# Wide attention: key blocks weighed in pairs, and all projections of a unit at its last block

## The chip, the cores and the metric

The kernel runs on one core of a Trainium2 chip. The metric is the device time of one launch in microseconds (us). The core has engines that run side by side and are ordered only by semaphores: TensorE (PE, matmuls into PSUM, with PEld for the loads of its stationary operand), VectorE (DVE), ScalarE (ACT), GpSimd (POOL), and SyncE (SP), which issues DMAs here.

## The reference

Four layers, each an attention-like part and a feed-forward part with layer norms between. The change touches the attention of the last layer alone ("wide": 16 heads of 64 channels, 4 sequences of 1024 tokens, 128 channels):

```python
def _L3_attn_ref(x, adaptive_scale, Wq, bq, Wk, bk, Wv, bv, Wo, bo, gamma, beta):
    H, HD, D = (16, 64, 128)
    Q = (x @ Wq.T + bq).reshape(B, N, H, HD)
    K = (x @ Wk.T + bk).reshape(B, N, H, HD)
    V = (x @ Wv.T + bv).reshape(B, N, H, HD)
    scores = jnp.einsum('bnhd,bmhd->bhnm', Q, K)
    scores = scores * (SCALE * adaptive_scale)[None, :, None, None] / TEMP
    w = jax.nn.softmax(scores, axis=-1)
    attn = jnp.einsum('bhnm,bmhd->bnhd', w, V).reshape(B, N, H * HD)
    y = x + (attn @ Wo.T + bo)
    ...                       # layer norm, times gamma, plus beta
```

## The kernel before

The wide stage is `wide_attention` (L4147). It works through 32 units, one for each sequence and pair of heads (4 x 8). The two heads of a pair lie in partitions 0 to 63 and 64 to 127. A unit has 8 key blocks (kb) of 128 keys, and each block two halves (h) of 512 queries.

One Python list, `plan`, sets the order of the work (L4234 to L4275). Every engine walks through the same list and does its own part of each step, so a step's place in the list is its place in each engine's queue. The steps:

- `score` (PE L4370 and L4373): for one block and half, the negated row maxima are added by a bf16 matmul with ones, then the fp32 product of keys and queries; two heads side by side (64 rows each). ScalarE takes the exponential of the whole tile (L4511) into one of 6 buffers.
- `max` (PE L4065, DVE L4096): bf16 scores of the *next* unit, and their maxima; 16 of them in a unit, spread over the blocks by `MAXIMA`.
- `weigh` (PE L4387): values times exponentials of one block, both halves, into two PSUM banks of its own that are kept through the unit; 64 output columns for each head.
- `add` (DVE, h = 0) and `add_beside` (POOL, h = 1), both L4304: the running sum of the exponentials. A list `waiting` holds the adds that GpSimd has still to do; `beside` takes one from it and puts it behind a `max`, for whose matmuls GpSimd then waits.
- `send` (DVE L4104, PE L4072, DVE L4109 and L4111, then four DMAs L4121): the negated maxima of the next unit, turned and stored as rows for its scores.
- `project_q`, `project_k` (PE L4056; ACT L4130, and L4139 with L4143) and `project_v` (PE L4051, DVE L4086): for the unit after the next.
- `keep` (ACT L4519), `sums` (PE L4398, ACT L4525, DMAs L4325), `invert` (DVE L4444, DMAs), `divide` (DVE L4439): the end of the unit before.
- `rows` (L269) and the norms' steps for a whole sequence: `next_step(True)` gives a heavy one, `next_step(False)` a light one. `gate_work` gives two pieces of the router's bisection (small VectorE steps, L3897 to L3963, `PIECES` = 9 + 8 x 25 + 6 of them) in each block but the last.

Three PSUM slots of two banks are handed round in turn by `with_banks` (L113): `score`, `max`, `send`, the projections, `sums`, `rows` and the turns each take the next one, and TensorE waits until the step that had it three takes before has been read out. An exponential waits until its buffer, used six tiles before, was weighed and added:

```python
if t >= E_BUFS:
    a_.wait_ge(*weighted.at(t - E_BUFS + 1))
    a_.wait_ge(*summed[t % HALF].at(add_of(t - E_BUFS)))
```

Of the kernel before, what the change touches and what calls it, by code (L numbers as in the profile page):

```python
# [10 lines left out]
NT = T // P  # L11
# [101 lines left out]
def with_banks(plan, n, released):  # L113


    out, done, at = [], [None] * n, -1
    for step in plan:
        if step[0] in released:
            at = (at + 1) % n
            out.append((step, at, done[at]))  # L120
            done[at] = released[step[0]](*step[1:])
        else:
            out.append((step, None, None))
    return out
# [3845 lines left out]
class WideHeads:  # L3970
# [3 lines left out]
    SLOTS, TILES, PRODUCTS, N_LOADS = 3, HALF * NT, 12, 8  # L3974
# [172 lines left out]
def wide_attention(core, heads, sort, tail):  # L4147
# [11 lines left out]
    own, units, SLOTS, TILES = heads.own, heads.units, heads.SLOTS, heads.TILES  # L4159
# [9 lines left out]
    sums = core.arena[:, ArenaBuffers.COLS - T - BANK:ArenaBuffers.COLS - T]  # L4169
# [31 lines left out]
    work, ends, later = [], [], []  # L4201
    rest = [moe.steps(1)] + [gathered(b) + moe.steps(b) for b in range(2, nb)]

    def gate_work(n):
        return [work.pop(0) for _ in range(min(n, len(work)))]

    def finish(b):
        ends.extend(("rows", 2 * b + i) for i in range(HALF))
        if b + 1 < nb:
            rest.insert(len(rest) - 1 if b == 0 else len(rest), [(False, None)] + mine.steps(b) +  # L4210
                        [(False, ("route",))] * (b == 0))
        else:
            later.extend([("stats_1", b), ("root_1", b), ("scale_1", b, 0), ("scale_1", b, 1),
                          ("affine", b, 0), ("affine", b, 1), ("affine", b, 2), ("stats_2", b),
                          ("root_2", b), ("scale_2", b, 0), ("scale_2", b, 1)])
            later.extend(("turn", 2 * b + i) for i in range(HALF))

    def next_step(heavy):

        while rest and not rest[0]:  # L4220
            rest.pop(0)
        if not rest or rest[0][0][0] != heavy:
            return []
        step = rest[0].pop(0)[1]
        if step == ("route",):
            work.extend([("gate",)] * Entmax.PIECES)
        return [step] if step else []

    waiting = []

    def beside(step):
        return [("add_beside", *waiting.pop(0), step)] if waiting else []

    plan = []  # L4234
    for u in range(len(units)):
        todo = list(range(TILES)) if u + 1 < len(units) else []
        for kb in range(NT):
            for h in range(HALF):
                plan.append(("score", u, kb, h))
                for _ in range((MAXIMA[kb] + h) // HALF if todo else 0):  # L4240
                    plan.append(("max", u + 1, todo.pop(0)))
                    plan += beside(plan[-1])
            plan += beside(None)
            if kb == NT - 1 and u + 1 < len(units):
                plan.append(("send", u + 1))
            if kb == NT - 1:
                more = u + 2 < len(units)
                plan += [("project_k", u + 2)] * more + next_step(True) + [("project_v", u + 2)] * more
            if kb:
                plan += [("weigh", u, kb - 1), ("add", u, kb)]  # L4250
                waiting.append((u, kb))
                if kb == NT - 2:
                    plan += next_step(True) + [("project_q", u + 2)] * (u + 2 < len(units))
            elif u:
                plan += [("weigh", u - 1, NT - 1), ("keep", u - 1)]
            if kb < NT - 1:
                plan += gate_work(IN_TILE)
            if kb < NT - 2:
                plan += next_step(False)
            if u and kb == 1:  # L4260
                plan.append(("sums", u - 1))
            elif u and kb == 3:
                plan.append(("invert", u - 1))
            elif u and kb == 5:
                plan.append(("divide", u - 1))
                if units[u - 1][1] == PAIRS - 1:
                    finish(units[u - 1][0])
            if kb >= NT - 2 and ends:
                plan.append(ends.pop(0))
    assert not work and not any(rest) and not ends  # L4270
    last = len(units) - 1
    plan += beside(None)
    plan += [("weigh", last, NT - 1), ("keep", last), ("sums", last), ("invert", last), ("divide", last)]
    finish(nb - 1)
    plan += ends + later  # L4275
    plan = with_banks(plan, 3, {
        "score": lambda u, kb, h: (exped, TILES * u + HALF * kb + h + 1),
        "sums": lambda u: (sums_kept, u + 1),
        "rows": lambda c: rows.left(c),
        "turn": lambda c: (turn.kept, c + 1),  # L4280
        "n_turn": lambda tag, c: (norms[tag].turn.kept, c + 1),
        "route": lambda: (entmax.router.done, 1), **heads.released()})
# [446 lines left out]
def build(nc, inp, const, out, n_batch):  # L4729
    core = Core()  # L4730
    core.nc, core.inp, core.const, core.out, core.n_batch = nc, inp, const, out, n_batch
    with ExitStack() as ctx:
# [49 lines left out]
        wide = WideHeads(core)  # L4782
        block_experts(core, sort, tail, wide)
        wide_attention(core, wide, sort, tail)
        wide.st.close()
        tail.st.close()
# [42 lines left out]
```

## Time and profile before

| | |
|---|---|
| median of 3 runs | 5642.71 us (5641.98 to 5645.2) |
| profiled execution, its own time | 5626.77 us |
| its span in the trace | 5625.0 us |
| TensorE busy | 5183.8 us (92%) |
| VectorE busy | 3972.7 us (71%) |
| ScalarE busy | 2760.5 us (49%) |
| GpSimd busy | 1340.1 us (24%) |
| wide stage | about 3593 to 5072 us |
| `score` exponentials, L4511 | 512 of 1.02 us |
| `max` reductions, L4096 | 496 of 1.22 us |

Busy times are unions of instructions of one engine. "Idle before" is the time in which an engine had nothing to do ahead of a group, with what ended it. TensorE's ends are modelled, so its pace is better read from the starts of its instructions; a wait of its own can stand with PEld, whose weight load goes first.

### The profile page before, as it was taken

How to read it: one execution, taken by the hardware profiler on the slowest of the kernel's cores; microseconds unless marked ns; L12 is line 12 of the kernel's file. 1: busy time of each engine (PE TensorE's matmuls, PEld its weight loads, DVE VectorE, ACT ScalarE, POOL GpSimd, SP SyncE). 2: the span in 40 equal slices, each digit the busy share in tenths (PEclk: the TensorE clock that was granted, in tenths of full speed). 3: DMA queues.
4: the chain of work that ended last, by engine and by line, in shares of the span. 5: the costliest groups of instructions: out<-in, count | busy, mean ns of one | idle time of the engine just before them, and what ended most of it. 6: DMA issues, size and time to landing. Idle time of an engine off the chain costs nothing. (4 is left out here: it accounts for less than half of the span.)

```text
span 5625.0 us, 103745 instructions
## 1 busy us (share of the span) xinstructions
PE 5183.8 (92%) x40013; PEld 2672.4 (48%) x40013; DVE 3972.7 (71%) x6826; ACT 2760.5 (49%) x4661; POOL 1340.1 (24%) x933
## 2 busy tenths in 40 slices
PE   6999997787999999998999979899999999997999
PEld 2333333444567777773333339433433434335676
DVE  7888886774567677777998944578688787864312
ACT  4767666221233333336786866454454454442333
POOL 0120100230112322322112214155344343440000
PEclk7999999787999999999999989999999999998999
DMA  4212110002111111111122113000000000001000
GB/s 91 49 33 32 33 32 12 0 0 63 37 33 25 30 26 30 26 30 31 27 39 38 42 51 88 29 20 17 13 13 20 9 13 13 13 16 35 5 5 8
DMA packets 148427, 158.08 MB, mean 28 GB/s; under 512 B 48980, under 2 KB 95108, under 8 KB 147508
## 3 DMA queue, kind: packets, MB, share of 16 engines
q1 hardware_dynamic: 143336, 142.37, 11.6%
q0 software_dynamic: 4096, 8.40, 0.5%
q8 instruction: 318, 5.21, 0.4%
q14 instruction: 173, 1.42, 0.1%
q10 hardware_dynamic: 504, 0.69, 0.1%
HBM read 118.20 MB, written 37.40 MB: 28 GB/s over the span
## 5 line engine op out<-in xcount | busy, mean ns | idle before, releaser
L4096 DVE TENSOR_REDUCE wide_max_parts<-wide_p 128x2 f32<-128x1024 f32 x496 | 595.2, 1220 | 130.0 <-PE wide_p L4065 117.9
L795 ACT ACTIVATE attn_w<-l_p 128x512 f32<-128x512 f32 x1024 | 553.4, 595 | 229.7 <-DVE l_p L1241 115.7
L2594 PE MATMUL caus_p<-caus_x_one,big 128*128 128x129 f32 x4608 | 634.1, 284 | 0.0
L641 DVE TENSOR_REDUCE l_max_parts<-l_p 128x2 f32<-128x1024 f32 x512 | 601.8, 1218 | 44.3 <-PE l_p L617 40.5
L2678 ACT ACTIVATE big<-caus_p 128x512 f32<-128x512 f32 (+3 forms) x768 | 345.9, 489 | 544.7 <-PE caus_p L2580 399.7
L641 DVE TENSOR_REDUCE rot_max_parts<-rot_p 128x2 f32<-128x1024 f32 x488 | 574.1, 1219 | 46.3 <-PE rot_p L617 43.1
L2594 PEld LDWEIGHTS caus_p<-caus_x_one,big 128*128 128x128 f32 x4608 | 585.1, 197 | 35.6 <-issue 2.3
L4373 PE MATMUL wide_p<-arena 64*128 64x512 f32 x2048 | 530.2, 596 | 0.0
L4511 ACT ACTIVATE attn_w<-wide_p 128x1024 f32<-128x1024 f32 x342 | 350.4, 1024 | 333.8 <-PE wide_p L4373 332.5
L4304 POOL TENSOR_TENSOR big<-big,attn_w 128x1024 f32<-128x1024 f32 x128 | 333.5, 2605 | 392.8 <-PE wide_p L4065 380.9
L641 DVE TENSOR_REDUCE caus_max_parts<-caus_p 128x2 f32<-128x1024 f32 (+2 forms) x360 | 340.4, 956 | 24.2 <-PE caus_p L617 15.9
L772 PE MATMUL l_p<-l_q_stack,l_k_stack 98*32 98x512 bf16 x4096 | 342.9, 388 | 5.8 <-ACT attn_w L795 4.2
L2712 POOL TENSOR_TENSOR attn_w<-attn_w,caus_part 128x256 f32<-128x256 f32 x256 | 185.7, 725 | 677.4 <-DVE caus_part L2652 677.4
L4387 PE MATMUL wide_p<-attn_w,arena 128*64 128x512 f32 x1368 | 332.0, 606 | 0.0
L772 PE MATMUL rot_p<-arena 98*32 98x512 bf16 x4096 | 319.6, 386 | 6.3 <-ACT big L795 2.1
L795 ACT ACTIVATE attn_w<-rot_p 128x512 f32<-128x512 f32 x512 | 275.5, 596 | 88.3 <-PE rot_p L772 87.6
L3333 ACT ACTIVATE arena<-moe_experts,moe_b 128x512 f32<-128x512 f32 x256 | 175.2, 687 | 271.4 <-PE moe_experts L3321 271.2
L795 ACT ACTIVATE big<-rot_p 128x512 f32<-128x512 f32 x512 | 274.5, 598 | 58.4 <-PE rot_p L772 55.1
L805 PE MATMUL l_p<-attn_w,l_v_one 128*32 128x512 f32 x2048 | 270.5, 605 | 0.0
L3354 DVE SCALAR_TENSOR_TENSOR x_mid<-moe_experts,last_gates,x_mid 128x128 f32<-128x128 f32 x256 | 72.1, 344 | 279.7 <-PE moe_experts L3343 279.6
L4511 ACT ACTIVATE wide_exps<-wide_p 128x1024 f32<-128x1024 f32 x170 | 174.2, 1024 | 161.2 <-PE wide_p L4373 160.5
L3321 PE MATMUL moe_experts<-x_chn,big 128*128 128x512 f32 x512 | 237.2, 606 | 14.1 <-ACT arena L3333 8.8
(645 smaller groups left out, 9016.8 us busy)
## 6 DMA issues: line engine op xcount, KB each, us to landing
arena<-q_parts SPq DMA_DIRECT2D x576, 32.0 KB
arena<-k_parts SPq DMA_DIRECT2D x576, 32.0 KB
arena<-inverse_rows SPq DMA_DIRECT2D x64, 256.0 KB
l_q_stack<-q_parts SPq DMA_DIRECT2D x279, 32.0 KB
l_k_stack<-k_parts SPq DMA_DIRECT2D x279, 32.0 KB
q_parts<-arena SPq DMA_DIRECT2D x8, 768.0 KB, 3.7
k_parts<-arena SPq DMA_DIRECT2D x8, 768.0 KB, 3.6
attn_w<-moe_in SPq DMA_DIRECT2D x19, 256.0 KB
```

Of the source, the lines that this page charges most:

```text
L641: self.nc.vector.tensor_reduce(self.max_parts[:, 2 * p:2 * p + 2, n, half], pair[:, :, 0:self.width(n, half)], AX.X, ALU.max).then_inc(*se ...
L772: mm = nc.tensor.matmul(bank[strip, :], heads.k_stack[i][0:STACK, j, kb * P + strip.start:kb * P + strip.stop], heads.q_stack[i][0:STACK, ...
L795: self.nc.scalar.activation(self.exps[t % len(self.exps)], bank, ACT.Exp).then_inc(*self.exped.up())
L805: mm = self.nc.tensor.matmul(self.out[self.W * j:self.W * (j + 1), :], self.v_one[u % 2][:, kb, j, :], self.exps[(t + j) % len(self.exps)] ...
L2594: mm = nc.tensor.matmul(outs[o % 2][:, nq % 2 * (C + 1):(nq % 2 + 1) * (C + 1)], exps[h % 2][:, kb, nq * P:(nq + 1) * P], x_one[b % 2][:, ...
L2678: nc.scalar.activation(exps[h % 2][:, kb, lo:BANK], bank[:, lo:BANK], ACT.Exp).then_inc(*exped.up())
L3321: self.nc.tensor.matmul(self.up_banks[o % 3], self.w1[:, e, c * P:(c + 1) * P], cols, start=True, stop=True).then_inc(*self.up_mm.up())
L4096: self.nc.vector.tensor_reduce(self.max_parts[:, :, n, h], side, AX.X, ALU.max).then_inc(*self.maxed.up())
L4304: calls.tensor_tensor(to, first, exps[t % E_BUFS], ALU.add).then_inc(*summed[h].up())
L4373: mm = nc.tensor.matmul(side[:, a, :], k[u % SLOTS][own[a], kb * P:(kb + 1) * P], q[u % SLOTS][own[a], cols], start=False, stop=True)
L4387: mm = nc.tensor.matmul(out[own[a], h, :], v_tok[u % SLOTS][:, kb, own[a]], exps[t % E_BUFS][:, a, :], start=kb == 0, stop=kb == NT - 1)
L4511: nc.scalar.activation(exps[t % E_BUFS], side, ACT.Exp).then_inc(*exped.up())
```

## The change

It only changes the order of the steps. `weigh` is no longer done for one block behind each block of scores. At kb 2, 4 and 6 the two blocks before are weighed together, at kb 0 the last two of the unit before. The adds of both blocks follow, and both of GpSimd's adds are put into `waiting` there. At the last block the order is project_k, send, project_q, a heavy step, project_v; then the rows steps of a finished sequence, both at once. sums, invert and divide stand one block later (2, 4, 6). GpSimd's adds are no longer emptied behind each block, only beside maxima.

```diff
     for u in range(len(units)):
-        todo = list(range(TILES)) if u + 1 < len(units) else []
+        todo, more = list(range(TILES)) if u + 1 < len(units) else [], u + 2 < len(units)
         for kb in range(NT):
             ...
-            plan += beside(None)
-            if kb == NT - 1 and u + 1 < len(units):
-                plan.append(("send", u + 1))
             if kb == NT - 1:
-                more = u + 2 < len(units)
-                plan += [("project_k", u + 2)] * more + next_step(True) + [("project_v", u + 2)] * more
-            if kb:
-                plan += [("weigh", u, kb - 1), ("add", u, kb)]
+                plan += [("project_k", u + 2)] * more
+                if u + 1 < len(units):
+                    plan.append(("send", u + 1))
+                plan += [("project_q", u + 2)] * more + next_step(True) + [("project_v", u + 2)] * more
+                plan += ends
+                ends.clear()
+            if kb % 2 == 0 and kb:
+                plan += [("weigh", u, kb - 2), ("weigh", u, kb - 1), ("add", u, kb - 1), ("add", u, kb)]
+                waiting += [(u, kb - 1), (u, kb)]
+                if kb == NT - 2:
+                    plan += next_step(True)
+            elif kb == NT - 1:
+                plan.append(("add", u, kb))
                 waiting.append((u, kb))
-                if kb == NT - 2:
-                    plan += next_step(True) + [("project_q", u + 2)] * (u + 2 < len(units))
-            elif u:
-                plan += [("weigh", u - 1, NT - 1), ("keep", u - 1)]
+            elif kb == 0 and u:
+                plan += [("weigh", u - 1, NT - 2), ("weigh", u - 1, NT - 1), ("keep", u - 1)]
             if kb < NT - 1:
                 plan += gate_work(IN_TILE)
             if kb < NT - 2:
                 plan += next_step(False)
-            if u and kb == 1:
+            if u and kb == 2:
                 plan.append(("sums", u - 1))
-            elif u and kb == 3:
+            elif u and kb == 4:
                 plan.append(("invert", u - 1))
-            elif u and kb == 5:
+            elif u and kb == 6:
                 plan.append(("divide", u - 1))
                 ...
-            if kb >= NT - 2 and ends:
-                plan.append(ends.pop(0))
     ...
-    plan += beside(None)
-    plan += [("weigh", last, NT - 1), ("keep", last), ("sums", last), ("invert", last), ("divide", last)]
+    while waiting:
+        plan += beside(None)
+    plan += [("weigh", last, NT - 2), ("weigh", last, NT - 1), ("keep", last), ("sums", last), ("invert", last),
+             ("divide", last)]
```

## Rows read from the trace of the kernel before

**Rows 1.** Windows of the wide stage: length, busy us (instructions) by engine, TensorE clock.
```profile
3700.00:3800.00 100.00, 99.91 (x520) 36.61 (x518) 78.81 (x98) 51.09 (x57) 49.45 (x25) 1.00 0.08 22
4300.00:4400.00 100.00, 93.88 (x530) 43.64 (x528) 76.38 (x122) 37.93 (x37) 32.24 (x13) 0.98 0.04 12
```

**Rows 2.** TensorE in order of time, one key block: start us, length, line, shape.
```profile
3786.09 0.38 PE L4065 MATMUL wide_p<-wide_k_bf,wide_q_bf 64*128 64x512 bf16 x2
3786.31 0.38 PE L4370 MATMUL wide_p<-wide_max_rows,wide_ones_bf 64*128 64x512 bf16 x2
...
3787.39 0.39 PE L4065 MATMUL wide_p<-wide_k_bf,wide_q_bf 64*128 64x512 bf16 x2
3787.71 1.94 PE L4387 MATMUL wide_p<-attn_w,arena 128*64 128x512 f32 x8
3789.58 0.39 PE L4370 MATMUL wide_p<-wide_max_rows,wide_ones_bf 64*128 64x512 bf16 x2
```

**Rows 3.** Order of time at kb 7 of one unit.
```profile
4564.90 1.02 PE L4373 MATMUL wide_p<-arena 64*128 64x512 f32 x4
...
4566.16 0.27 PE L4072 MATMUL wide_p<-ident,wide_neg_max 128*16 128x128 f32 x1 [0.24 <-DVE wide_neg_max L4104]
4566.27 1.88 PE L4056 MATMUL wide_p<-x_chn,big 128*128 128x512 f32 x4
...
4567.99 1.95 PE L4051 MATMUL wide_p<-big,x_chn 128*128 128x128 f32 x16
4568.19 1.11 ACT L4139 ACTIVATE arena<-wide_p,wide_bk 128x1024 f32<-128x1024 f32 x1 [1.19 <-PE wide_p L4056]
...
4569.20 1.11 ACT L4143 ACTIVATE wide_k_bf<-wide_p,wide_bk 128x1024 bf16<-128x1024 f32 x1
...
4569.87 1.94 PE L4387 MATMUL wide_p<-attn_w,arena 128*64 128x512 f32 x8
4569.98 1.23 DVE L4086 TENSOR_TENSOR arena<-wide_p,wide_bv 128x1024 f32<-128x1024 f32 x1 [1.85 <-PE wide_p L4051]
4571.12 1.21 DVE L4304 TENSOR_TENSOR big<-big,wide_exps 128x1024 f32<-128x1024 f32 x1
```

**Rows 4.** Order of time around the last unit's first scores.
```profile
5030.78 0.28 PE L4072 MATMUL wide_p<-ident,wide_neg_max 128*16 128x128 f32 x1
...
5035.69 0.39 PE L4370 MATMUL wide_p<-wide_max_rows,wide_ones_bf 64*128 64x512 bf16 x2 [2.75 <-DMA wide_max_rows<-wide_max_lo]
...
5037.13 1.95 PE L4373 MATMUL wide_p<-arena 64*128 64x512 f32 x4
```

**Rows 5.** Order of time at kb 0, with two maxima steps in a row at 3771.86.
```profile
3770.57 0.38 PE L4065 MATMUL wide_p<-wide_k_bf,wide_q_bf 64*128 64x512 bf16 x2
...
3770.99 3.66 DVE L4096 TENSOR_REDUCE wide_max_parts<-wide_p 128x2 f32<-128x1024 f32 x3 [0.91 <-PE wide_p L4065]
...
3771.04 2.35 POOL L4304 TENSOR_TENSOR big<-big,attn_w 128x1024 f32<-128x1024 f32 x1 [8.60 <-PE wide_p L4065]
...
3772.27 0.10 PEld L4065 LDWEIGHTS wide_p<-wide_k_bf,wide_q_bf 64*128 64x128 bf16 x2 [0.32 <-DVE wide_max_parts L4096]
```

**Rows 6.** Order of time where a router piece meets GpSimd.
```profile
4597.99 3.35 POOL L4304 TENSOR_TENSOR big<-big,attn_w 128x1024 f32<-128x1024 f32 x1
...
4599.05 2.32 DVE L3951 COPY_PREDICATED wide_ent_low<-wide_ent_keep,wide_ent_mid 128x8 f32<-128x8 uint32 x1
...
4604.85 0.60 PE L4370 MATMUL wide_p<-wide_max_rows,wide_ones_bf 64*128 64x512 bf16 x2 [3.83 <-DVE wide_max_parts L4096]
```

**Rows 7.** TensorE's waits in the stage: us in total, times, longest.
```profile
PE wide_p L4370 <- DVE wide_max_parts L4096: 17.2, 8, 3.8
PE wide_p L4056 <- DVE wide_max_parts L4096: 8.7, 5, 2.4
PE wide_p L4072 <- DVE wide_neg_max L4104: 7.4, 18, 1.0
```

## The prediction

> **What bounds the kernel now.** I read the windows of the wide stage first [rows 1]: TensorE is busy 94 to 100 of every 100 us, VectorE 76 to 79, ScalarE 38 to 51. The stage lasts from about 3593 to 5072 us, 32 units of some 46 us. So TensorE sets the end, VectorE is near behind it, and all that this change can give is TensorE time. Then the time order of TensorE in one key block [rows 2]. Two starts are to be compared: a weigh step begins 0.32 us after the maxima step ahead of it, where the same maxima step takes 0.22 us when scores follow. And the weigh step holds TensorE for 1.87 us, where its eight passes, run in pairs, should take 1.72 (four single passes of a projection take that, 4566.27 to 4567.99 [rows 3]). Entering and leaving the weigh step thus costs 0.10 + 0.15 = 0.25 us, some 0.125 for each change between the shapes 64*128, 128*64 and 128*128. That is time at full busy share: it cannot be seen in the busy rows, only in the starts.
>
> The Trainium skill (TensorEngine Tiling (Array Packing), Key Properties) says that changing the tiling mode drains the engine. This trace agrees with 0.25 us a visit; by that rule alone the change would be faster, and this is the first rival below.
>
> **What the change removes.** In a unit the shape changes 19 times now: kb 0 twice, kb 1 three times (weigh, sums, scores), kb 2 to 5 twice each, kb 6 three times (project_q), kb 7 three times. After it: kb 0 twice, kb 2 three times, kb 4 and 6 twice, kb 7 twice, 11 in all. 8 x 0.125 = 1.0 us a unit, x 31 = -31 us. The send step now stands behind project_k. Before, it came right behind the scores and waited for the negated maxima (0.24 us in one unit [rows 3], 18 waits of 7.4 us in all [rows 7]): -7 us, bounds 0 and -9 (0.3 in each).
>
> **What it costs, part by part.** There are three PSUM slots, taken in turn: each step that takes a slot waits for the release of the third take before it. All that follows comes from that.
>
> (a) Rows of maxima. SyncE issues four DMAs behind the send; the next unit's first scores wait for the last. In the one unit where nothing covers them, scores follow the send by 4.90 us, 2.75 of it idle [rows 4]. Now project_k, project_v and a weigh cover it [rows 3]. After the change project_k stands ahead of the send and the weigh moved behind the scores, so what is left between is send 0.11, project_q 1.72, project_v 1.88: 3.7 us [rows 3]. TensorE waits 1.2 us. Part of that would be lost anyway: project_v takes the slot of project_k, which ScalarE starts to read 1.92 us behind the start of its matmuls (0.1 more behind a change of shape) and reads in two passes of 1.11 [rows 3]; the slot is free 2.5 us behind the send, 0.6 too late. The two waits are in series and together still end at 4.90. Of 31 units, 30 have projections and 3 are followed by the 7 us rows steps: 27 x 1.2 = 32, less 2 for units with a step between: +30. The last such unit loses the cover of a weigh: +2.
>
> (b) VectorE behind project_v. It adds the bias 1.99 us after project_v starts, 1.23 us, then add kb 7, 1.21 us [rows 3]; the weigh that covered this is gone. From the send at 0: project_v at 2.5, values 4.5 to 5.7, add to 6.9, first maxima reduced 6.9 to 8.1. The first maxima are made at 6.0 and the third maxima step takes their slot; undisturbed that comes 1.71 us later, at 7.7. Now it comes at 8.2: 0.5 x 27 = +14 us.
>
> (c) The queue of exponentials against GpSimd. Exponential t overwrites the buffer of t - 6 and so waits for the add that reads it. Exponentials of kb 3, second half, need GpSimd's add of kb 1. Today that add runs beside the maxima of kb 2. After the change it is put in the queue only behind kb 2, and starts beside the first maxima of kb 3: 0.47 us after their start, for 2.35 us [rows 5]. So the exponential starts 2.9 us after that maxima step, ends at 3.9, and the slot is free at 4.0. The slot is wanted by the first maxima of kb 4, 2.8 us after it (two scores, one maxima, and (d)). TensorE waits 1.2 us in each unit: x 31 = +37 us. The same late add at kb 0 is harmless: a weigh pair of 3.6 us stands between.
>
> (d) Two blocks with no weigh between. A slot taken by a maxima step is free 1.71 us after its start (0.42 to the reduction, 1.22 for it, 0.07 back); TensorE comes back to it after maxima, scores, maxima: 1.51. Today this shows where two maxima steps follow each other [rows 5]: the second is released by the reduction. After the change the third scores of kb 1-2, 3-4 and 5-6 meet it too: 3 x 0.2 x 31 = +19 us.
>
> (e) Small VectorE steps under GpSimd. Some 215 router pieces, two in a block, fill 15 units. Today they stand behind the adds, when GpSimd has mostly finished. At kb 3 and kb 5 they will stand between the reductions of the two blocks, where GpSimd's second queued add runs (from 0.47 + 2.35 us on, for 2.35). What that does is shown at 4599 us [rows 6]: a piece of 0.16 us takes 2.32, since it ends only with GpSimd's operation, and TensorE then idles 3.83 us for a slot. Here it delays the reductions by some 2.3 us, which the weigh pair hides in part; the adds and the inversion behind it reach into the next block's first reduction: 1.1 us there and 0.5 at the send. Bounds 0 and 1.6 a unit; I take half, 0.8 x 15 = +12 us.
>
> The Trainium skill (SBUF — State Buffer, two separate sides) says that one of GpSimd and VectorE holds the shared port for a whole instruction and the other blocks. The rows agree. Taken at its full extent it would put (e) at 24 us and the time at 5731.
>
> Other moved steps: sums, invert and divide go one block later; VectorE does them behind the adds of a weigh pair, hidden. SyncE's transfers for them keep their order and distance (two blocks each). The rows steps stand together at kb 7; their TensorE time is the same. The waits behind weigh steps of today (17.2 and 8.7 us [rows 7]) come from GpSimd's long steps under VectorE; they will move, not go. I leave them, bound 26 us less or as much more.
>
> **Sum.** -31 - 7 + 30 + 2 + 14 + 37 + 19 + 12 = +76 us. The profiled execution has a span of 5625.0 us and a time of 5626.8; 5626.8 + 76 = 5703. The median of the runs lies 15.9 above that execution, so 5719 us, 1.3% slower.
>
> **Rivals.**
> 1. The drains decide and the waits are absorbed: (a) to (e) come to nothing, only -38 is left: 5605. For it: TensorE is 94 to 100% busy and every step still has its producer earlier in order. Against it: (a) and (c) are dependences with measured lengths, and the DMA wait has happened once [rows 4]. Chance 0.06. It is the case if less than 1.2 us a unit is lost.
> 2. Half of it: the waits overlap more than I count, (a) and (c) each at a third, (d) and (e) gone: 10 + 12 (of 30 and 37) - 38, which gives 5627, or even with (b) too, 5641. Chance 0.06.
> 3. Waits add up with the clock. After the 2.75 us idle wait the passes of the second scores took 1.95 us together, where they take 1.02 [rows 4], and the granted clock of a window with such waits is 0.98 rather than 1.00 [rows 1]: TensorE falls to 1.2 GHz, of its 2.4. If the 1.2 us waits at kb 7 and kb 4 each cost one such 0.9 us in every unit, that is 2 x 0.9 x 31 = 56 more, 5775. Against it: they are under half as long as that wait, and TensorE is busy for 15 us or more between them. Chance 0.13.
> 4. The forecast, between 5680 and 5750: chance 0.75.
>
> The range takes in most of 3 and the lower part between 2 and 4: 5660 to 5775. About 0.2% (11 us) is what a measurement here tells from no change. Faster than 5631: 0.08; between 5631 and 5654: 0.05; slower: 0.87.
>
> **What would show it.** In the changed trace, in an ordinary unit: a maxima step ahead of a weigh pair at 0.32 and the pair together 3.6 us, not 3.74 (removal right). Scores 4.9 us behind the send, with a DMA named as what ended the wait (a). ScalarE's exponential at the second half of kb 3 waiting for GpSimd (c), with TensorE's first maxima of kb 4 some 4.0 us behind the first of kb 3. The third scores of each pair of blocks 1.7 us behind the first maxima (d). Router pieces of 2.3 us at odd blocks between 4290 and 5000 us (e). Units some 2 us longer each. I am wrong if ScalarE doesn't wait for GpSimd there, or if the rows land sooner than 3.7 us behind the send.

## The result and the profile after

The changed kernel takes 5823.32 us (median of 5 runs, 5809.45 to 5825.16) against 5642.71 before; the ratio is 1.0319, 95% interval 1.0305 to 1.0332. The prediction was 5719 with a range of 5660 to 5775: the sign was right, the time lies above the range, and the loss is 181 us where 76 was forecast. The profiled execution has a span of 5823.4 us, 198 more than the one of before; 18 of these lie ahead of the stage, which starts at 3609 us there and at 3591 before.

The whole wide stage first, one window of the kernel before and one of the changed kernel (columns: length, busy us and instructions of PE, PEld, DVE, ACT and POOL, then the granted TensorE clock, DMA share, GB/s):

```profile
3593.00:5072.00 1479.00, 1441.20 (x7551) 554.85 (x7549) 1144.09 (x1531) 717.27 (x772) 653.15 (x274) 0.99 0.06 15
```

```profile
3593.00:5260.00 1667.00, 1468.17 (x7547) 579.41 (x7548) 1207.34 (x1529) 708.11 (x775) 614.12 (x271) 0.97 0.05 13
```

These two windows don't cut the stage at the same steps. From the first score step to the last, TensorE is busy 1439.7 of 1477.5 us before and 1465.9 of 1658.8 after. So the stage is some 181 us longer, TensorE's idle time went from 38 to 193 us, and it is also busy 26 us longer for the same work with fewer changes of shape, at a clock of 0.97 instead of 0.99.

What it waited for, from the waits view of TensorE in the stage (us in total, times, longest); [rows 7] is what answers to it before:

```profile
PE wide_p L4051 <- ACT wide_k_bf L4143: 66.3, 30, 2.2
PE wide_p L4065 <- DVE wide_max_parts L4096: 32.5, 28, 2.7
PE wide_p L4065 <- ACT attn_w L4515: 28.2, 28, 1.1
PE wide_p L4374 <- DVE wide_max_parts L4096: 27.0, 19, 3.4
PE wide_p L4065 <- ACT wide_exps L4515: 15.1, 15, 1.1
PE wide_p L4072 <- DVE wide_neg_max L4104: 9.2, 9, 5.4
```

(The changed kernel's lines from the plan on are 4 higher: L4374 is L4370 of before, L4377 is L4373, L4391 is L4387, L4515 is L4511. In the kernels of the experiments the same steps stand up to 9 lines behind those of before.)

The first row was in the prediction with 0.6 us a unit, some 18 us, and not with 66. The third and the fifth, 43 waits of some 1 us, are for the most part item (c): with GpSimd's adds queued block by block (below) 15 of them with 12.1 us stay. To place the rest, I took from the time order the start of each first score step of kb 0, 1, 3, 5 and 7 and made differences. Sums over the first 31 units, and one unit without norms or router pieces (the third), in us:

| stretch | before, sum | after, sum | before, one unit | after, one unit |
|---|---|---|---|---|
| kb 0 | 157.2 | 259.7 | 4.98 | 7.56 |
| kb 1 and 2 | 326.3 | 348.9 | 10.54 | 10.48 |
| kb 3 and 4 | 291.0 | 342.4 | 9.13 | 10.28 |
| kb 5 and 6 | 396.2 | 289.4 | 11.05 | 9.07 |
| kb 7 | 274.2 | 384.3 | 7.94 | 10.26 |
| all | 1444.9 | 1624.7 | 43.65 | 47.66 |

(kb 0 has a weigh step more after the change and kb 7 one less; project_q went from kb 6 to kb 7, and so did some rows steps.) The plain unit lost 4.0 us; x 31 that is 124 of the 180. The other 56 us lie in units with norms or router pieces, or with a lowered clock; the plain one ran at full clock in both kernels.

Kb 7 and the start of kb 0 in one unit of the changed kernel, in order of time; it answers to [rows 3]:

```profile
3744.69 1.98 PE L4056 MATMUL wide_p<-x_chn,big 128*128 128x512 f32 x4
...
3746.51 0.27 PE L4072 MATMUL wide_p<-ident,wide_neg_max 128*16 128x128 f32 x1
3746.62 1.88 PE L4056 MATMUL wide_p<-x_chn,big 128*128 128x512 f32 x4
...
3748.54 1.11 ACT L4139 ACTIVATE arena<-wide_p,wide_bk 128x1024 f32<-128x1024 f32 x1 [2.71 <-PE wide_p L4056]
...
3749.56 1.11 ACT L4143 ACTIVATE wide_k_bf<-wide_p,wide_bk 128x1024 bf16<-128x1024 f32 x1
...
3750.72 2.05 PE L4051 MATMUL wide_p<-big,x_chn 128*128 128x128 f32 x16 [2.21 <-ACT wide_k_bf L4143]
...
3752.70 0.39 PE L4374 MATMUL wide_p<-wide_max_rows,wide_ones_bf 64*128 64x512 bf16 x2
...
3754.25 2.35 POOL L4308 TENSOR_TENSOR big<-big,attn_w 128x1024 f32<-128x1024 f32 x1 [14.46 <-PE wide_p L4065]
3754.57 3.11 DVE L4308 TENSOR_TENSOR big<-big,wide_exps 128x1024 f32<-128x1024 f32 x1
...
3758.87 0.39 PE L4065 MATMUL wide_p<-wide_k_bf,wide_q_bf 64*128 64x512 bf16 x2 [2.70 <-DVE wide_max_parts L4096]
```

ScalarE reads project_k 3.85 us behind its start, not 2.02: it waits 2.71 us, and what ends that is the *next* L4056, project_q. The cause stands in the code, in a function that the diff doesn't touch: `projected` counts products in the order of execution, and project_k's read waits for `PRODUCTS * u + 4`. Where q comes first that is "q and k are done"; where k comes first it is "k and also q are done". Nothing breaks, it is only late. So scores follow the send by 6.19 us, not 4.90. Then, at kb 0 of this unit, VectorE's add begins 0.3 us behind the first of three GpSimd adds, takes 3.11 us instead of 1.21, and the third maxima waits 2.70 us. It is one of the seven units whose kb 0 takes 10 to 12 us; in most it takes 7.56.

Item (c) in the same trace, kb 3 of the next unit:

```profile
3774.62 0.38 PE L4065 MATMUL wide_p<-wide_k_bf,wide_q_bf 64*128 64x512 bf16 x2
...
3775.09 2.34 POOL L4308 TENSOR_TENSOR big<-attn_w 128x1024 f32<-128x1024 f32 x1 [12.67 <-PE wide_p L4065]
...
3777.55 1.02 ACT L4515 ACTIVATE attn_w<-wide_p 128x1024 f32<-128x1024 f32 x1 [1.69 <-POOL big L4308]
...
3778.62 0.39 PE L4065 MATMUL wide_p<-wide_k_bf,wide_q_bf 64*128 64x512 bf16 x2 [1.05 <-ACT attn_w L4515]
```

The exponential starts 2.93 us behind the first maxima step, and the first maxima of kb 4 stands 4.00 us behind it: both as predicted.

### The profile page after: what moved, and what is told of

Its sections match the earlier page's. It is cut to its first block and busy times, and to the rows that moved or that the text cites. A ratio compares the mean times of both kernels' runs of the same rounds, so it can differ in the third digit from the quotient of the medians.

```text
span 5823.4 us, 103746 instructions
## 1 busy us (share of the span) xinstructions
PE 5215.8 (90%) x40013; PEld 2695.8 (46%) x40013; DVE 4042.1 (69%) x6826; ACT 2751.0 (47%) x4661; POOL 1306.9 (22%) x933
## 5 line engine op out<-in xcount | busy, mean ns | idle before, releaser
L4515 ACT ACTIVATE attn_w<-wide_p 128x1024 f32<-128x1024 f32 x342 | 348.1, 1022 | 424.5 <-PE wide_p L4377 343.4
L4377 PE MATMUL wide_p<-arena 64*128 64x512 f32 x2048 | 536.3, 603 | 0.0
L4308 POOL TENSOR_TENSOR big<-big,attn_w 128x1024 f32<-128x1024 f32 x128 | 316.5, 2473 | 462.8 <-PE wide_p L4065 443.6
L4391 PE MATMUL wide_p<-attn_w,arena 128*64 128x512 f32 x1368 | 322.3, 603 | 0.0
L4515 ACT ACTIVATE wide_exps<-wide_p 128x1024 f32<-128x1024 f32 x170 | 173.4, 1023 | 218.0 <-PE wide_p L4377 179.6
L4065 PE MATMUL wide_p<-wide_k_bf,wide_q_bf 64*128 64x512 bf16 x992 | 192.0, 385 | 76.8 <-DVE wide_max_parts L4096 32.5
```

What stands on the lines that cost most here:

```text
L4308: calls.tensor_tensor(to, first, exps[t % E_BUFS], ALU.add).then_inc(*summed[h].up())
L4377: mm = nc.tensor.matmul(side[:, a, :], k[u % SLOTS][own[a], kb * P:(kb + 1) * P], q[u % SLOTS][own[a], cols], start=False, stop=True)
L4391: mm = nc.tensor.matmul(out[own[a], h, :], v_tok[u % SLOTS][:, kb, own[a]], exps[t % E_BUFS][:, a, :], start=kb == 0, stop=kb == NT - 1)
L4515: nc.scalar.activation(exps[t % E_BUFS], side, ACT.Exp).then_inc(*exped.up())
```

## The experiments

The first question was how the 181 us divide: the count, GpSimd's queue, and what is left.

**The count alone.** The changed kernel, and in `project_q_on_act` and `project_k_on_act`:

```diff
-        a_.wait_ge(*self.projected.at(self.PRODUCTS * u + 2))          # q
+        a_.wait_ge(*self.projected.at(self.PRODUCTS * u + (2 if u < 2 else 4)))
-        a_.wait_ge(*self.projected.at(self.PRODUCTS * u + 4))          # k
+        a_.wait_ge(*self.projected.at(self.PRODUCTS * u + (4 if u < 2 else 2)))
```

> The changed kernel with only the two thresholds of the counting semaphore swapped for the units projected at the last block: ScalarE's read of project_k waits for the first two products of the unit (it is now first on TensorE), that of project_q for four. Theory A (order against count: today project_k's read waits until project_q's matmuls are done too, project_v then waits 2.4 us for the slot): project_v's wait falls from 2.4 to 0.6 us, scores follow the send by 4.9 us (the rows' DMAs) and not 6.2, 1.3 us x 27 units = 35 us less, about 5788 us. Rival (VectorE's values, add and first reduction are what kb 0 waits for anyway): under 10 us less, the wait only moves to the third maxima of kb 0.

Measured: 5750.75 us, ratio to before 1.0199 (1.0172 to 1.0225): 73 us less than the change, twice what was expected. Its kb 7:

```profile
3738.24 0.27 PE L4072 MATMUL wide_p<-ident,wide_neg_max 128*16 128x128 f32 x1
...
3738.44 1.11 ACT L4139 ACTIVATE arena<-wide_p,wide_bk 128x1024 f32<-128x1024 f32 x1 [0.88 <-PE wide_p L4056]
...
3740.61 2.05 PE L4051 MATMUL wide_p<-big,x_chn 128*128 128x128 f32 x16 [0.38 <-ACT wide_k_bf L4143]
...
3743.14 0.39 PE L4374 MATMUL wide_p<-wide_max_rows,wide_ones_bf 64*128 64x512 bf16 x2 [0.48 <-DMA wide_max_rows<-wide_max_lo]
...
3744.47 1.21 DVE L4308 TENSOR_TENSOR big<-big,wide_exps 128x1024 f32<-128x1024 f32 x1
...
3744.69 3.20 POOL L4308 TENSOR_TENSOR big<-big,attn_w 128x1024 f32<-128x1024 f32 x1 [13.16 <-PE wide_p L4065]
```

Scores follow the send by 4.90 us with the DMA named. That is item (a) as written down, once the count is right. Kb 7 sums to 327.5 us (384.3 in the change), kb 0 to 228.3 (259.7), where the units of 10 and 12 us are now 7.1 to 7.8; kb 1 and 2 take 17 us back (365.9, from 348.9). In the unit above VectorE now comes to kb 0 ahead of GpSimd: its add starts 0.22 us first and takes 1.21 us, and GpSimd's beside it takes 3.20.

The plain third unit takes 45.85 us here, 2.2 more than before. The prediction's terms for such a unit give 2.3: -1.0 - 0.2 + 1.2 + 0.5 + 1.2 + 0.6. So the missed count is the whole of the miss in a plain unit: 47.66 us with it, 45.85 without.

**GpSimd's adds block by block.** The changed kernel, with `waiting` filled at each block and emptied behind its scores:

```diff
-                waiting += [(u, kb - 1), (u, kb)]
...
+            if kb:
+                waiting.append((u, kb))
```

> The changed kernel, but GpSimd's adds are queued one block each, beside the maxima of the next block and emptied at each block's end, as in the kernel before; weigh pairs, VectorE's adds and projections stay as changed. Theory A (two costs of the paired GpSimd adds: the exponential of kb 3 second half waits 1.7 us for GpSimd, 1.15 us of TensorE a unit, and three adds in a row at kb 0 hold VectorE's add and router steps up): kb 3-4 falls from 10.3 to 9.1 us, the units with 10 or 12 us at kb 0 fall to 7.6; 36 + 30 to 50 us less, about 5745 us. Rival (only the wait of the exponential counts): 36 us less, 5787, with kb 0 unchanged.

Measured: 5769.56 us, ratio 1.024 (1.022 to 1.026): 54 us less. Kb 3 and 4 fall to 9.07 us in a plain unit (296.1 in sum, from 342.4), so (c) is 1.21 us a unit, and kb 1 and 2 lose another 20. Kb 0 fell by only 12 us (247.4), where theory A had 30 to 50, and kb 7, where the count's wait of 66.3 us stands as before, grew by 15 (399.3).

**Both.**

> Both edits together on the changed kernel: thresholds swapped, GpSimd's adds queued block by block. Theory A (the costs lie in different blocks and add up): about 5710 us, what the prediction had for the rest: rows' DMAs 1.2 us and third maxima 0.5 to 0.9 a unit, three times 0.2. Rival (they share a chain at kb 0): 5740 or more.

Measured: 5672.41 us, ratio 1.0065 (1.0047 to 1.0083). It is 151 us less than the change, more than 73 + 54, and 38 less than theory A: either wait hides part of what the other costs, and together the edits also end nearly all of the clock's losses. Its stage:

```profile
3593.00:5105.00 1512.00, 1419.70 (x7531) 557.08 (x7533) 1170.44 (x1529) 710.64 (x771) 634.28 (x271) 1.00 0.06 15
```

From the first score step to the last, the same TensorE work takes 1422.4 us here at clock 1.00 and 1465.9 in the changed kernel at 0.97: 43 us more. The clock can also be added up directly, as time x (1 - granted clock) over that stretch of each trace. It falls short of full clock by 15 us in the kernel before and 46 in the changed one, by 20 with the count alone put right, 46 with GpSimd's queue alone and 5 with both. The 41 us between the last and the changed kernel are near the 43 of busy time. So by these sums, an estimate, since TensorE was idle for a part of the slow time, the clock holds some 31 of the change's 181 us, and 26 of them go with the count. Against the kernel before, 17 us less busy don't test the -31 us for the changes of shape, since up to 10 of them can be the clock; the starts of the steps do (below).

**The weigh pairs alone**, on the kernel before (and two weigh steps together at kb 0 and at the very end):

```diff
             if kb:
-                plan += [("weigh", u, kb - 1), ("add", u, kb)]
+                if kb % 2 == 0:
+                    plan += [("weigh", u, kb - 2), ("weigh", u, kb - 1)]
+                plan.append(("add", u, kb))
```

> The kernel before with one part of the change alone: blocks weighed in pairs at kb 2, 4, 6 and 0. Projections, adds, GpSimd's queue, sums, invert and divide stay as before. 6 changes of shape fewer in a unit, 0.75 us x 31 = 23 us. Theory A (a weigh step is also cover for transfers and VectorE): without the weigh behind project_v, scores wait 1.2 us for the rows' DMAs and the third maxima of kb 0 some 0.5 us, two third scores 0.2 each: 2.1 us x 31 = +65 us, net about 5680 us. Rival (only the drains count): 5620 us.

Measured: 5752.69 us, ratio 1.0199 (1.0175 to 1.0222), 72 more than theory A. Its waits:

```profile
PE wide_p L4372 <- DVE wide_max_parts L4096: 53.7, 27, 5.1
PE wide_p L4372 <- DMA wide_max_rows<-wide_max_lo: 34.1, 28, 4.6
PE wide_p L4056 <- DVE wide_max_parts L4096: 15.6, 13, 2.8
```

34.1 us for the rows' DMAs is what theory A had (1.2 x 28). The larger part, 69 us for VectorE's reductions where the kernel before has 26 [rows 7], it had not, and blocks 5 and 6 alone sum to 449.0 us, from 396.2. VectorE's add of the odd block now stands in the dense stretch between the weigh pairs, and where it meets a GpSimd step it takes longer, and the reductions behind it come late. One unit, at kb 5 and 6:

```profile
3687.86 2.36 POOL L3500 TENSOR_TENSOR x_mid<-x_mid,tail_be 128x1024 f32<-128x1024 f32 x1
3687.96 3.35 DVE L4306 TENSOR_TENSOR big<-big,attn_w 128x1024 f32<-128x1024 f32 x1
...
3694.53 2.34 DVE L4096 TENSOR_REDUCE wide_max_parts<-wide_p 128x2 f32<-128x1024 f32 x2
...
3695.80 2.62 PE L4056 MATMUL wide_p<-x_chn,big 128*128 128x512 f32 x4 [2.65 <-DVE wide_max_parts L4096]
```

Kb 0 of a plain unit is 6.69 us, that of before and one weigh step more: theory A's 0.5 us at the third maxima did not come. The stage's clock is 0.97 here too, without any wait for the count. The rival fell altogether.

**The projections alone**, on the kernel before, in the order of the change (project_k, send, project_q, heavy step, project_v), with single weigh steps:

> The kernel before with the other part of the change alone: project_k, send, project_q, heavy step, project_v at the last block; one weigh step behind each block of scores as before. Theory A (the read of project_k waits for the count that project_q completes, so project_v waits 2.4 us in each unit whatever the weigh steps do): one change of shape fewer, -0.13, 0.2 less at the send, +2.4 a unit in 30 units, kb 7 from 7.9 to about 12 us with kb 6 1.9 less, net +60 to +70 us: about 5700. With the clock falling after such waits, up to 40 more. Rival (the wait comes only with the pairs): about 5630.

Measured: 5733.01 us, ratio 1.0161 (1.0145 to 1.0176), +92. The same wait, 66.3 us in 30 times, without any pairs. And the clock can be read off (time order, then two windows of the same unit):

```profile
3742.24 2.71 PE L4051 MATMUL wide_p<-big,x_chn 128*128 128x128 f32 x16 [2.21 <-ACT wide_k_bf L4143]
3744.88 2.90 PE L4388 MATMUL wide_p<-attn_w,arena 128*64 128x512 f32 x8
...
3743.00:3747.00 4.00, 4.00 (x18) 2.42 (x18) 3.68 (x11) 0.28 (x1) 0.00 (x0) 0.57 0.02 4
3747.00:3760.00 13.00, 12.98 (x74) 4.32 (x72) 9.48 (x20) 6.14 (x7) 2.55 (x2) 1.00 0.00 1
```

After 2.21 us of idle the granted clock is 0.57 over the next 4 us, most of them at 1.2 GHz, and project_v and weigh take 2.71 and 2.90 us where they take 1.95 and 1.94 [rows 3]. Kb 7 is some 13.7 us in such units and 12.1 in the few where it doesn't happen: 1.6 us. It doesn't follow every such wait. All 30 waits are 2.21 us long, and project_v took 2.5 to 3.7 us instead of 2.05 behind 23 of them here, but behind 15 of 30 in the changed kernel and 21 of 30 with GpSimd's queue alone. The unit of the changed kernel shown above is one where it did not.

**The send first**, to give the transfer its cover back, on the kernel with GpSimd's adds block by block (here q comes before k, so the counts are right as they are):

```diff
-                plan += [("project_k", u + 2)] * more
                 if u + 1 < len(units):
                     plan.append(("send", u + 1))
-                plan += [("project_q", u + 2)] * more + next_step(True) + [("project_v", u + 2)] * more
+                plan += [("project_q", u + 2)] * more + next_step(True) + [("project_k", u + 2)] * more
+                plan += [("project_v", u + 2)] * more
```

> The changed kernel with GpSimd's adds queued block by block, and at kb 7 the order send, project_q, a heavy step, project_k, project_v (thresholds as in the kernel before, which fit this order). Theory A (the transfer of the rows, 4.9 us behind the send, wants cover): send to scores is now 0.1 + 1.7 + 1.7 + 1.9 = 5.4 us of own work, no DMA wait, and project_v takes the slot of a step that is long free; kb 7 falls from 9.5 us (both edits) to about 8.1, 1.4 us x 27 = 38 us less than that kernel's 5672: 5635. Rival (VectorE's values, add and first reduction come later behind the scores and take it back at kb 0): kb 0 grows from 6.7-7.6 to 7.6-8.4, about 5660.

Measured: 5710.91 us, ratio 1.0127 (1.0107 to 1.0147), 38 us *more* than with both edits. The rival saw a part: kb 0 of a plain unit is 7.56 us, 12 more in sum. Kb 7 grew by 35, which neither theory had: the wait for the DMA is gone, and in its place stands

```profile
PE wide_p L4072 <- DVE wide_neg_max L4104: 66.0, 31, 2.9
```

VectorE has two adds, perhaps a heavy step, and divide to do between the last maxima and the negated maxima; project_k had covered that (13.6 us of waits there with both edits).

**The add first.** As above, with ("add", u, 7) ahead of project_v.

> As the kernel with the send first, and VectorE's add of kb 7 put ahead of project_v, so that only the values stand between project_v and the first reduction of kb 0. Theory A: kb 0 falls to its own work, 6.7 us, and the kernel comes to about 5630, even with the kernel before or 0.2% faster: 8 changes of shape fewer (31 us) against three waits of 0.2 us a unit (19 us). Rival (the add is not on the path): same as the kernel with the send first.

Measured: 5681.42 us, ratio 1.008 (1.0059 to 1.01). Kb 0 fell from 7.56 to 6.70 us in a plain unit, its own work, 23 us in sum. This is item (b): 0.86 us in a plain unit of this order. In the change's own order, with both edits made, kb 0 sums to 222.7 us against 207.7 for the pairs alone: 15 us, where 14 had been forecast. The total missed theory A by 51 us; the 66.0 us of waits at the send are still there.

**Half of the maxima's work left out**, to test item (d): in the kernel with the add first and in the kernel before, the reduction reads `side[:, :, 0:BANK // 2]`.

> As the kernel with the add first, but each reduction of maxima reads only the first half of its columns (half of the maxima's work is left out; 0.7 us in place of 1.2). Theory A (between two weigh pairs the third scores wait 0.2 us for the slot of the first maxima, because a reduction and its two hand-overs take 1.7 us and TensorE is back in 1.5): the blocks 3-4 and 5-6 fall from 9.07 to 8.87 us each and 1-2 from 10.48 to 10.08, and VectorE is never late; 5590 us or less. Rival (the pair costs 9.07 us for a reason in TensorE): 9.07 stays.

> The kernel before with the same half reductions (half of the maxima's work is left out). The control for the one before: only the two waits between adjacent maxima steps go, 0.2 us each, and part of the 26 us of waits for VectorE: blocks 3-4 stay at 9.13 us, 1-2 fall from 10.54 to 10.34; about 5610 us. If blocks 3-4 are 9.13 here and 8.87 with pairs, a weigh pair is worth 0.25 us, the full price of two changes of shape. Rival: 3-4 fall here too.

Measured: 5646.02 us (ratio 1.0018, 1.0005 to 1.0031) and 5608.23 (0.9944, 0.9924 to 0.9964). The first is 56 us above theory A, with 64.0 us of waits at the send still in it; the second is as expected. Item (d) is read from the blocks, not from the totals. Blocks 3 and 4, from the first scores of kb 3 to those of kb 5: 9.13 us in the kernel before and 9.13 with half maxima; 9.07 with weigh pairs and 8.88 with pairs and half maxima. In the time order of the kernel with both edits, full maxima:

```profile
3708.76 0.39 PE L4375 MATMUL wide_p<-wide_max_rows,wide_ones_bf 64*128 64x512 bf16 x2
...
3709.84 0.38 PE L4065 MATMUL wide_p<-wide_k_bf,wide_q_bf 64*128 64x512 bf16 x2
...
3710.26 2.53 DVE L4096 TENSOR_REDUCE wide_max_parts<-wide_p 128x2 f32<-128x1024 f32 x2 [1.57 <-PE wide_p L4065]
...
3711.13 0.39 PE L4065 MATMUL wide_p<-wide_k_bf,wide_q_bf 64*128 64x512 bf16 x2
...
3711.55 0.39 PE L4375 MATMUL wide_p<-wide_max_rows,wide_ones_bf 64*128 64x512 bf16 x2
...
3714.24 3.65 PE L4392 MATMUL wide_p<-attn_w,arena 128*64 128x512 f32 x16
...
3717.83 0.39 PE L4375 MATMUL wide_p<-wide_max_rows,wide_ones_bf 64*128 64x512 bf16 x2
```

and the kernel with half maxima:

```profile
3701.27 0.38 PE L4065 MATMUL wide_p<-wide_k_bf,wide_q_bf 64*128 64x512 bf16 x2
...
3702.56 0.39 PE L4065 MATMUL wide_p<-wide_k_bf,wide_q_bf 64*128 64x512 bf16 x2
3702.79 0.38 PE L4375 MATMUL wide_p<-wide_max_rows,wide_ones_bf 64*128 64x512 bf16 x2
```

The third scores start 0.42 us behind the second maxima step in the first and 0.23 in the second: 1.71 us behind the first maxima step, when its reduction has been handed back, as predicted. The weigh pair itself holds TensorE for 3.59 us (3714.24 to 3717.83) where two single steps take 3.74 [rows 2]. So two blocks gain 0.25 us by the pair, and 0.19 of it is given back at once at the third scores. The cost of a change of shape was priced right, and with the whole reductions and this order of maxima and scores there was never more than 0.06 us in a pair of blocks to be had.

**Divide late**, and the heavy step of kb 6 at kb 4, on the kernel with the add first:

> As the kernel with the add first (5681 us), with divide moved from kb 6 to behind project_k of kb 7, and the heavy step of kb 6 moved to kb 4: nothing but adds and router pieces stands on VectorE between the last maxima and the negated maxima of the send. Theory A (there TensorE waits 66 us in 31 sends): most of it goes, kb 7 falls from 10.3 to about 8.3 us, 5681 - 50 to 60 = 5625 us, even with the kernel before. Rival (VectorE has no room at kb 7 either: divide, add and values come late for kb 0): kb 0 grows by as much, about 5670.

Measured: 5660.14 us, ratio 1.0038 (1.0024 to 1.0051), the best form with pairs that does all of the work. Kb 7 fell to 7.84 us in a plain unit (299.4 in sum, from 365.5), and kb 0, 1-2 and 5-6 grew by 24, 10 and 10: the rival held in part. In its waits view the 66.0 us at the send are 13.6, and TensorE's scores wait 28.3 us for the values (L4086) and 15.2 for reductions.

**Maxima apart**, on that kernel, so that a maxima step's slot comes round after two scores (one list for each block: 0 and 1 are its two halves of scores, M is a maxima step):

```diff
+    ORDER = [[0, M, 1, M, M], [M, 0, M, 1], [M, 0, 1, M, M], [M, 0, 1, M], [0, 1, M, M], [M, 0, 1, M],
+             [0, 1, M, M], [0, 1]]
```

> As the kernel with divide late, with maxima and scores in another order between two weigh pairs: maxima, two scores, maxima, two scores, two maxima, so that a slot taken by a maxima step comes round again after two scores (2.4 us) and not after scores and maxima (1.5). Theory A (0.2 us a pair of blocks goes): blocks 3-4 and 5-6 fall from 9.07 to 8.87 us, 15 to 20 us less than the kernel with divide late: about 5608, 0.5% under the kernel before. Rival (VectorE gets its reductions in a bunch beside the adds and the first maxima behind a weigh pair waits): 9.1 us or more stay.

Measured: 5767.11 us, ratio 1.0237 (1.0218 to 1.0255). Blocks 3 and 4 do take 8.88 us in plain units, as theory A said. But kb 5 and 6 take 10.4 in the third unit (9.07 with the change) and up to 16.8 in others:

```profile
3824.36 3.35 DVE L3387 SCALAR_TENSOR_TENSOR x_mid<-x_mid,sort_top_m 128x128 f32<-128x128 f32 x4
...
3829.69 0.61 PE L4065 MATMUL wide_p<-wide_k_bf,wide_q_bf 64*128 64x512 bf16 x2 [3.85 <-DVE wide_max_parts L4096]
```

A maxima step in front of the scores of a block asks VectorE for a reduction just when it is behind with the adds of the pair or, as here, with a heavy step beside a GpSimd add. TensorE waited 3.85 us, and its next passes took 0.61 us where they take 0.38. This order is all that differs from the kernel with divide late, and maxima steps wait 79.4 us for reductions here and 1.8 there; that the meeting at VectorE makes the wait is read from single units.

**One last version without pairs**: the kernel before, and at kb 7 send, project_q, heavy step, project_k, project_v, weigh.

> The kernel before with single weigh steps, and project_q moved to the last block in an order that fits the counts and the slots: send, project_q, heavy step, project_k, project_v, weigh. Theory A (all that the change could give without losing the cover of the weigh steps): one change of shape fewer, 0.13 x 30 = 4 us; project_q no longer waits at kb 6 for VectorE's slot, up to 9 us; the send can't wait behind project_k: about 5630 us, 0.1 to 0.2% faster than before. Rival (1.7 us more of projections behind the send push VectorE's values and add into kb 0, as with the send first and pairs): 5650 or more, with 0.5 us and more at kb 0.

Measured: 5640.45 us, ratio 1.0009 (0.9997 to 1.002): no difference. No version that does all of the work was found to beat the kernel before.

## Why the prediction was right in sign and wrong in size

The step that failed is in (a): the prediction took it that ScalarE starts to read project_k 1.92 us behind its matmuls, whatever stands behind it, and so had project_v wait 0.6 us. The read came at 3.85 us, behind project_q, and project_v waited 2.21 us in each of 30 units. With only the count put right the kernel takes 5750.75 us, which is inside the range. Taken one after the other, the 181 us are 73 for the count, 78 for GpSimd's queue (5750.75 to 5672.41; 54 when it is undone alone) and 34 over the kernel before, which took 5638.4 us in those runs. In the sum the count stood with nothing, the queue with the 37 of (c), and all the rest with 39.

- **Changes of shape, -31 us: right where it was measured.** A pair takes 3.59 us and not 3.74; blocks 3 and 4 with half maxima are 8.88 against 9.13. The two changes of shape of the projections were not measured apart.
- **(a), +30 us: the step that failed.** The sentence "ScalarE starts to read 1.92 us behind the start of its matmuls" carried a duration of the old order into the new one. The wait in the code is for a count of products, and with project_k first it is met only by project_q. Scores came 6.2 us behind the send, not 4.9: 1.3 us more in each of the units that the 30 us were made of, some 35 us. With the thresholds swapped the 4.90 us came out. The other half of the 73 us shows in the clock and at kb 0, where VectorE comes earlier with the count put right.
- **The clock, left at a chance of 0.13: nothing in the sum, some 31 us by its records.** It was priced for waits of 1.2 us, and those hardly lowered it: with the count put right, and (c) still in place, it falls short of full clock by 20 us, and by 15 before. The wait of 2.21 us that the missed count made was followed by slow passes in half of the changed kernel's units, and 26 of the 31 us go with the count. But the pairs alone have a clock of 0.97 as well, with waits of up to 5.1 us for reductions and none for the count: the count is not the only thing that lowers it.
- **(b), +14 us: too low.** I took the add of kb 7 at 1.21 us. Where GpSimd's first add starts ahead of it, it takes 3.11. Kb 0 of plain units was 7.56 us, against some 7.2 by my times; seven of 31 units had 10 to 12. In sum kb 0 lies 102 us over before; 53 of these are the weigh step that moved there, and (b) and this contention the remaining 49. Of the 49, 31 go with the count and another 6 with the queue; the 12 that stay are near (b) as forecast. The prediction called GpSimd's late adds at kb 0 harmless, for the exponentials; that one of them would hold VectorE's add up stood in no term.
- **(c), +37 us: right in its mechanism and near in size.** 1.05 us in the trace, 1.21 in a plain unit, 46.3 us fewer at kb 3 and 4 with the queue undone. The queue's other cost, 20 us at kb 1 and 2 and 12 at kb 0, was in no term of its own.
- **(d), +19 us: right**, 0.19 us a pair of blocks, read at blocks 3 and 4.
- **(e), +12 us: not told apart.** The 56 us outside the plain part hold it, the contention at kb 0 and the clock.
- **-7 us at the send: wrong,** 9.2 us of waits there after against 7.4.
- Rival 1 (the drains decide) fell in each form: no kernel with pairs that does all of the work was below 1.0038.

That the sign came out right is not luck, since (c) and (d) and the DMA wait of (a) were found as written down. What stays open is how the last 56 us divide. By the clock's records some 31 of them are the clock's; the others, router pieces and adds under GpSimd, no run takes apart.

## What to carry to other kernels

Before a step is moved, read what the waits on it count: a semaphore that counts completions names a position in the old order, and after a swap it names another step's end, correct and late. Price a cheaper step on the bottleneck engine together with what runs under it: here each weigh step gave a transfer, a reduction and an add their time, and of 0.25 us gained 0.19 was owed at the next slot. And look at the clock behind a repeated wait on a busy engine: here one of 2.2 us cost up to 1.6 us more, in half of the units or in most of them, by the order of the rest.

## What the runs showed of the hardware

- After 2.21 us of idle TensorE's granted clock was 0.57 over the next 4 us and 1.00 over the 13 us behind (the projections alone). The same wait was followed by slow passes 23 times of 30 there and 15 times of 30 in the changed kernel. With waits up to 1.2 us in nearly every unit (both edits) the stage's clock was 1.00.
- Entering the shape 128*64 from 64*128 cost 0.10 us and the visit another 0.15, with fp32 passes in the weigh step (two blocks 9.13 to 8.88 us with one visit fewer); a second weigh step of another block behind the first cost none (3.59 us for the pair, twice 1.72 and 0.15).
- Of VectorE's adds with two SBUF inputs, 22 in the changed kernel's stage started while a GpSimd operation ran. The 15 with 1.3 us or more of it to go ended 1.1 us behind its end (2.4 to 3.3 us in all, for 1.21); the 7 with 0.7 us or less to go took 1.2. The reductions from PSUM beside GpSimd never took over 1.23 us (some 250 of them). Where VectorE's add started 0.22 us first it took 1.21 us, and GpSimd's 3.20: which of them is first decides up to 2 us.
